# Silu of queries, keys and values as one ScalarE function into SBUF, with two gate results issued earlier

## The reference

```python
qkv = jax.nn.silu(hidden_states @ qkv_w.T)        # silu(a) = a * sigmoid(a); then q, k, v of each head
# per head: scores = (q k^T) * decay, causal; attended = scores v
normed = norm_w * attended * rsqrt(mean(attended ** 2) + eps)
gate = jax.nn.sigmoid(hidden_states @ gate_w.T)
out = gate * normed @ out_w.T
```

## Time and profile before

| | |
|---|---|
| time, median of 3 runs (range) | 1873.34 us (1871.03 to 1873.51) |
| span of the profiled execution, first to last instruction | 1870.5 us |
| own time of the profiled execution | not recorded apart; its span is 2.84 us under the median |
| TensorE busy | 1807.6 us (97%) |
| VectorE busy | 1443.7 us (77%) |
| ScalarE busy | 940.1 us (50%) |
| GpSimd busy | 627.6 us (34%) |
| chain that ended last: TensorE, VectorE, ScalarE | 77%, 13%, 4% |
| TensorE's granted clock, mean | 0.992 |

### The profile page before, as it was taken

The page is one execution under the profiler, slowest core; times in us unless marked ns, Lnnn a source line. Parts: engine busy times, 40 slices in busy tenths (PEclk is TensorE's granted clock), DMA queues, the critical chain, the costliest instruction groups (busy, mean ns, idle before and its releaser), DMA issues.

```text
span 1870.5 us, 26340 instructions
## 1 busy us (share of the span) xinstructions
PE 1807.6 (97%) x9325; PEld 872.7 (47%) x9325; DVE 1443.7 (77%) x2029; ACT 940.1 (50%) x1402; POOL 627.6 (34%) x506
## 2 busy tenths in 40 slices
PE   6999999999999999999999999999999999998887
PEld 4444544444444544444444544444444544564433
DVE  7777777778777777778777777778777777669877
ACT  5554544545454545545454545445354544434664
POOL 2352334324342334324342334324342332301423
PEclk9999999999999999999999999999999999999998
DMA  4112223131322223221321213121221213133332
GB/s 174 65 68 91 69 90 90 69 90 46 119 63 90 69 89 91 76 83 46 119 62 57 70 56 90 57 68 46 85 63 57 71 54 91 58 103 122 113 91 90
DMA packets 117792, 149.64 MB, mean 80 GB/s; under 512 B 67232, under 2 KB 83744, under 8 KB 117280
## 3 DMA queue, kind: packets, MB, share of 16 engines
q1 hardware_dynamic: 106208, 135.29, 22.9%
q0 software_dynamic: 2560, 8.39, 1.4%
q10 hardware_dynamic: 8896, 4.28, 0.8%
HBM read 119.63 MB, written 12.58 MB: 71 GB/s over the span
## 4 chain that ended last, share of the span: by engine, by line
PE 77%; DVE 13%; ACT 4%; issue 4%; DMA 1%; POOL 0%; ACTq 0%; DVEq 0%; SPq 0%; POOLq 0%
PE bank L1296 18%; PE bank L1298 17%; PE bank L1297 17%; PE bank L1269 6%; PE bank L1361 4%; PE bank L1363 3%; PE bank L1362 3%; DVE gated_split L1616 3%; PE bank L1338 2%; PE bank L1340 2%; PE bank L1339 2%; DVE acc L1758 2%; PE bank L1425 1%; PE bank L1436 1%; DVE bank L1676 1%
## 5 line engine op out<-in xcount | busy, mean ns | idle before, releaser
L1296 PE MATMUL bank<-x_blocks,w_pair 128*128 128x512 f16 (+1 forms) x1820 | 678.5, 373 | 12.7 <-DVE bank L1664 7.3
L1298 PE MATMUL bank<-x_blocks,w_pair 128*128 128x512 f16 (+1 forms) x1820 | 678.3, 373 | 0.0
L1297 PE MATMUL bank<-x_blocks,w_pair 128*128 128x512 f16 (+1 forms) x1820 | 678.2, 373 | 0.0
L1876 POOL TENSOR_TENSOR sums_pair<-raw_pair 128x512 f32<-128x512 f32 x63 | 87.0, 1380 | 576.5 <-DVE w_pair L1616 414.6
L1296 PEld LDWEIGHTS bank<-x_blocks,w_pair 128*128 128x128 f16 x1820 | 177.9, 98 | 218.2 <-DVE bank L1664 15.0
L1298 PEld LDWEIGHTS bank<-x_blocks,w_pair 128*128 128x128 f16 x1820 | 178.0, 98 | 202.8
L1297 PEld LDWEIGHTS bank<-x_blocks,w_pair 128*128 128x128 f16 x1820 | 178.1, 98 | 191.0
L1758 DVE TENSOR_TENSOR acc<-acc,bank 128x512 f32<-128x512 f32 x320 | 207.8, 680 | 17.5 <-PE bank L1363 17.5
L1537 ACT ACTIVATE scores_split<-bank 128x512 f16<-128x512 f32 (+1 forms) x192 | 100.6, 526 | 180.9 <-DVE bank L1721 160.7
L1616 DVE SCALAR_TENSOR_TENSOR w_pair<-raw_pair,w_pair 128x1024 f16<-128x1024 f32 x126 | 158.0, 1273 | 34.3 <-ACT w_pair L1489 34.1
L1902 POOL TENSOR_TENSOR ssq<-ssq,sig 128x512 f32<-128x512 f32 x64 | 83.4, 1303 | 282.4 <-ACT sig L1543 281.9
(11 more groups left out here) (212 smaller groups left out, 2637.4 us busy)
## 6 DMA issues: line engine op xcount, KB each, us to landing
raw_pair<-w_qk SPq DMA_DIRECT2D x32, 1024.0 KB, 5.0
raw_pair<-w_gate SPq DMA_DIRECT2D x16, 1024.0 KB, 4.9
raw_pair<-w_out SPq DMA_DIRECT2D x16, 1024.0 KB, 4.9
raw_pair<-w_vt SPq DMA_DIRECT2D x15, 1024.0 KB, 4.9
decay_sb<-decay SPq DMA_DIRECT2D x32, 256.0 KB, 5.3
raw_pair<-ctx_in SPq DMA_DIRECT2D x8, 1024.0 KB, 4.8
acc<-x_t SPq DMA_DIRECT2D x4, 1024.0 KB, 11.5
ctx<-raw_pair SPq DMA_DIRECT2D x8, 512.0 KB, 3.4
```

The source lines that it names most:

```text
L1296: pe.matmul(out, w_hi, x_hi, start=unmet and k == 0, stop=False, skip_group_check=halves or not fresh)
L1297: pe.matmul(out, w_hi, x_lo, start=False, stop=False, skip_group_check=halves or not fresh)
L1298: mm = pe.matmul(out, w_lo, x_hi, start=False, stop=k == QT - 1, skip_group_check=halves or not fresh)
```

## The change

The Silu of a q, k or v quarter becomes one ScalarE instruction, the function Silu, from bank or `p_copy` into the fp32 SBUF tile `sig`. The multiplication on VectorE is gone. High and low half are made from `sig` instead of from the bank. The bank is released once Silu has read it; the `sig` tile is held until the low half is made. Besides, the last two gate results of a pair (`gate_rest`: gate(3), gate(2)) move from after product 6 of the query stage to after product 1, ahead of unit 3's split and of the first query result. The pair n = 15 had them there before. `kv_out`, `v_out` and `end_v` change as `qk_out` does below.

```diff
@@ def silu(self, done, place, sign, dst, dst_free):
-        st = self.add("silu", done=done, place=place, sign=sign, gi=gi, sig_free=self.sig_free[gi], sig=self.tick("sig"),
-                      silu=self.tick("silu"), dst=dst, free=dst_free if isinstance(dst_free, list) else [dst_free],
+        st = self.add("silu", done=done, place=place, sign=sign, gi=gi, sig_free=self.sig_free[gi], silu=self.tick("silu"),
+                      dst=dst, free=dst_free if isinstance(dst_free, list) else [dst_free],
                       slot=self.late_slot, hi=self.tick("qkv_hi"))
-        self.sig_free[gi] = st["silu"]
-        return self.tick("qkv_lo")
+        lo = self.sig_free[gi] = self.tick("qkv_lo")
+        return st["silu"], lo
@@ def qk_out(self, which, r):
-        lo = self.silu(done, place, sign, (which, r), [self.qk_free, self.g_split] if which == "k" else self.qk_free)
-        self.release(place, lo)
+        silu, lo = self.silu(done, place, sign, (which, r), [self.qk_free, self.g_split] if which == "k" else self.qk_free)
+        self.release(place, silu)
@@ main_part, query stage of pairs 1 to 14
-            "p1": [attend(3), gated(3)] + units(3),
+            "p1": [attend(3), gated(3)] + gate_rest + units(3),
             "p2": sums(S2) + split_sum(S2) + stages(0) + sums(S1),
-            "p6": stages(1) + split_sum(S1) + sums(S4) + gate_rest + split_sum(S4),
+            "p6": stages(1) + split_sum(S1) + sums(S4) + split_sum(S4),
@@ scalar_program
         elif kind == "silu":
-            src = c.placed(st["place"])
             act.wait_ge(sem[st["done"][0]], st["done"][1])
             until(act, sem, st["sig_free"])
-            act.activation(c.sig32[st["gi"]][:, :], src, ACT.Sigmoid, scale=st["sign"] / W_SCALE).then_inc(sem["sig"])
+            act.activation(c.sig32[st["gi"]][:, :], c.placed(st["place"]), ACT.Silu,
+                           scale=st["sign"] / W_SCALE).then_inc(sem["silu"])
+            src = c.sig32[st["gi"]][:, :]
             act.wait_ge(sem["silu"], st["silu"][1])
@@ vector_program
         elif kind == "silu":
-            src = c.placed(st["place"])
-            dve.wait_ge(sem["sig"], st["sig"][1])
-            dve.scalar_tensor_tensor(out=src, in0=src, scalar=st["sign"] / W_SCALE, in1=c.sig32[st["gi"]][:, :],
-                                     op0=ALU.mult, op1=ALU.mult).then_inc(sem["silu"])
+            src = c.sig32[st["gi"]][:, :]
             dve.wait_ge(sem["qkv_hi"], st["hi"][1])
```

More of the change, by code:

```diff
@@ L63 @@
 SEMAPHORES = (
-    ["const_in", "ones_set", "constants", "quant_set", "x_hi", "x_lo", "w_hi", "w_lo", "sig", "silu", "qkv_hi", "qkv_lo",
+    ["const_in", "ones_set", "constants", "quant_set", "x_hi", "x_lo", "w_hi", "w_lo", "silu", "qkv_hi", "qkv_lo",
      "gate_sig", "score_mm", "decayed", "s_hi", "s_lo", "attend_mm", "sq", "gated", "g_sum", "g_hi", "g_lo", "ssq", "out_mm", "out_seeded",
@@ L340, in kv_out @@
         done, place, sign = self.result(r)
-        lo = self.silu(done, place, sign, ("kv", b, r), [self.qk_free, self.g_split, self.late_units_free])
-        self.release(place, lo)
+        silu, lo = self.silu(done, place, sign, ("kv", b, r), [self.qk_free, self.g_split, self.late_units_free])
+        self.release(place, silu)
         self.qk_done[("k", r // 2, b)] = lo
@@ L351, in v_out @@
         done, place, sign = self.result(r)
-        lo = self.silu(done, place, sign, ("v_unit", r), self.s_free if r == 0 else self.vo_free)
-        self.release(place, lo)
+        silu, lo = self.silu(done, place, sign, ("v_unit", r), self.s_free if r == 0 else self.vo_free)
+        self.release(place, silu)
         self.add("v_turn", r=r, ready=lo, free=max(self.v_hl_free))
@@ L386, in end_v @@
         bank = v["banks"][half]
-        done = self.silu(v["mm"][half], bank, 1.0, ("v", v["b"], half), self.v_hl_free[v["b"]])
+        silu, done = self.silu(v["mm"][half], bank, 1.0, ("v", v["b"], half), self.v_hl_free[v["b"]])
         self.v_done[v["b"]] = [[done]] * GH
-        self.main_ring.give(bank, done)
+        self.main_ring.give(bank, silu)
     def values(self, b):
```

## The result

The changed kernel takes 1891.59 us (median of 4 runs, 1890.04 to 1892.46) against 1872.31 for the kernel before on the same chip: ratio 1.0102, 95% interval 1.0088 to 1.0116. The forecast was 1895, 1.2% slower, with a range of 1870 to 1905. VectorE lost 87.6 us of busy time and TensorE did the same work; the kernel became 19 us slower. The 192 multiplications alone were 133 us, so the VectorE instructions that stay took some 45 us longer. TensorE's granted clock is no part of the 19 us: it is 0.992 on average in both, and ahead of the last 20 us it stood at its lower level, 1.2 GHz, for 13.7 us in all in each of the two profiled executions.

The account below looks back on a forecast made before the run. TensorE, busy 97% of the span, was taken as the bound, its waits set by VectorE's order of work. (2.1 - 0.43) x 14 = +23.4, less 1.3, gives +22; 1870.5 + 22 + 2.84 = 1895 us, range 1870 to 1905.

Parts of the forecast that it names:

- Table loads: ScalarE, before gate 0, q0 and gates 2 to 15: 30 more loads, 39 us of ScalarE; gate loads hidden.
- Rival (a): Silu shares Sigmoid's table set, no added loads, GpSimd turns stay: +0.4 to +0.9 us a pair, 1877 to 1885; chance 0.15.
- rival (d): A change of table costs twice its row, draining included: 1.28 x 14 us more, 1913; chance 0.05.
- Turns with GpSimd: Query stage: VectorE splits with both inputs in SBUF alternate with GpSimd's instructions; product 5 starts 2.1 us later per pair.
- The sign named for it: TensorE's wait for u3 grows from 0.45 to over 2 us a pair, some at the out product behind S2's split.
- Key stage and last pair: Key stage: wait for line 1758 goes, -0.43 x 14 = -6.0 us; last pair's seed wait: -1.3 us.
- The sum: (2.1 - 0.43) x 14 = +23.4, less 1.3: +22 us on the span of 1870.5.
- The last stretch: Last pair: a seed costs TensorE 2.14 us, its high half waited 1.42 for the multiplication; gain -1.3 us.
- Rival (b): Loads added, but low halves keep 0.69 us: (0.34 - 0.43) x 14 - 1.3 = -2.6, 1871; chance 0.13.
- Rival (c): Neither loads nor GpSimd turns: product 5 0.28 us sooner, key stage's 0.43 gone, -11 us, 1862; chance 0.10.
- The move: Query stage: two gate results wait for unit 3's gating; alone expected at +0.5 to +1.3 us a pair, 1879 to 1891.

Follow-up runs that it names:

- in-place kernel: The changed kernel with Silu written back into the PSUM bank (or copy of product 7) it reads, both halves made from there: 1864.09 us, ratio 0.9956.
- the kernel with both: The changed kernel with the activation written back where it reads, and Sigmoid where Silu stands (multiplication by the argument left out): 1861.61 us, ratio 0.9946.
- the kernel with only q0 in place: The changed kernel with only the first query quarter of pairs 1 to 15 written back into its bank and split there: 1868.87 us, ratio 0.9979.

## Why the prediction was right, point by point

- **Table loads: right.** 30 more, at the places named (Silu's line is 1524 in the changed kernel, not 1525), 1.283 us each, the next activation 0.01 to 0.02 us behind. Rival (a)'s set and rival (d)'s doubling are out. No draining of 1.38 us, as the Trainium skill has it (ScalarE: Activation LUTs, "What ACT_TABLE_LOAD costs"), is to be seen: the load's whole effect on the chain was 6.95 - 5.54 = 1.41 us, the load and the 0.1 us by which neighbouring activations otherwise overlap. The load before the gate results was hidden, as said: the Square after it had no idle time before it any more, but started in time.
- **Turns with GpSimd: right in kind.** q0's low half took 1.21 us, S2's split 1.75, and with the bank as source 0.69 and 0.68. With the order of the prediction, product 5 was to start 2.1 us later; it was 13.97 - 12.06 = 1.91. The steps on the way fit: in the clock of before, S2's split ended at 1083.65 (forecast 1083.6), the three additions at 1085.45 (1085.4), u3 at 1088.96 (1089.2). The sign named for it, a wait for u3 of over 2 us with some of it at S2, came with other shares: 0.30 at the seed, 1.15 at S2, 0.57 at u3, 2.0 in all.
- **Key stage and last pair: right.** The wait for line 1758 is gone (-0.43 us a pair), the last seed wait fell from 2.14 to 0.67 us, -1.5 for -1.3.
- **The sum:** (1.91 - 0.43) x 14 = +20.7, for +23.4 predicted. One term was missing and one sized too small:
- **Before pair 1, not in the sum.** The changed kernel is 1.9 us late: TensorE waits there 2.42 us for c22 at 56.61, after ScalarE waited 3.35 for GpSimd's first weight sums. It was 1.44 us in the in-place kernel. The rows of VectorE and GpSimd show turns again, of another split: without the multiplications VectorE reaches two splits of weights, both inputs in SBUF, 2.5 us sooner (47.04, before 49.57), beside GpSimd's sums. They take 4.48 us for 2.83 before (3.51 in place), GpSimd's last two sums 2.13 each for 1.27. No run moves these splits alone.
- **The last stretch, sized too small.** From pair 15 on it gave back 4.9 us by difference (17.4 = 1.9 + 20.4 - 4.9), of which the seed is 1.5. Of the other 3.4, some 2.6 stand at line 1269, where TensorE waited 3.5 us behind VectorE before and 0.9 now; multiplications left VectorE there too. The rest are small waits in both directions.
- **How near 1895 came.** In spans the forecast was +22.1 and the result +17.4: the pairs cost 3.0 less and the last stretch gave back 3.6 more than forecast, against the 1.9 before pair 1. That 1895 came as near as 3.4 us is in part luck: these errors cancel in part, and the new median lies 3.7 us above its profiled span where I added 2.84.
- **Rival (a), priced wrong.** I gave no loads with turns 1877 to 1885; measured 1868.08. S2's split was right (1082.4 against 1075.05 + 7.18 = 1082.23), the step behind it was not. The prediction doesn't write it out; for product 5 at 1087.9 or later, S1's and S4's splits had to meet one GpSimd sum more than before; it started at 1075.05 + 12.43 = 1087.48, as the two splits took 2.86 us for 2.87. What remained, +0.37 - 0.43, is nothing, and the end gave the rest.
- **Rival (b), right in kind.** Loads with low halves of 0.69 us: +0.34 - 0.43 a pair predicted, +0.18 - 0.43 measured; 1871 for 1864.09, the difference mostly in the same last stretch.
- **Rival (c): the number met, by another way.** Neither load nor turns is the kernel with both: 1861.61 for 1862. But product 5 started only 0.04 us sooner, not 0.28, as S4's split still stood ahead of u3; a pair won 0.50 us, not 0.71, and the last stretch gave the rest. With S4's split behind u3 product 5 did start 0.24 sooner (11.82 after the Square).
- **The move: overpriced** where I took it by itself (1879 or more, 1874.74 measured), since the split that it delays drops out of GpSimd's way. The forecast's own working had this 0.69, and was right.

## What to carry to other kernels

Price a delay against the moment at which its result is wanted, and all delays on one chain together: here each of two fitted into 1.4 us of slack and cost some 2 and 6.5 us in all, the pair of them 29, and both fitted again once the moved gate results went back. An instruction saved on a busy engine is worth what the bound engine waited for it, while the instructions that stay may get slower by their new operands: where a low half moves from PSUM to SBUF, look at what GpSimd does at that moment. If functions of two table sets must alternate, put the change where ScalarE idles anyway, even at the price of one old-style operation; here the number of loads (1, 31 or 59) didn't set the time, their places did.

## What the runs showed of the hardware that I had not expected

A table load doesn't wait for the data of the activation it stands before: it ran 3.46 us ahead of it (978.47 and 981.93 above). And the values' first quarter, its low half now with both inputs in SBUF, took 1.70 us in each of the 14 pairs, where GpSimd's sums ran beside it. It cost nothing: the kernel with only q0 in place keeps it, and its pairs are as long as with all in place (instructions on tile sig, changed kernel: count, shortest/median/longest ns):

```profile
L1617 DVE SCALAR_TENSOR_TENSOR scores_split<-sig,scores_split x14: 1695/1699/1704, 192.2 to 1578.2; 128x512 f16<-128x512 f32 x14
L1617 DVE SCALAR_TENSOR_TENSOR w_vo<-sig,w_vo x42: 691/692/693, 201.7 to 1592.1; 128x512 f16<-128x512 f32 x42
```

The 42 others of the value stage, with GpSimd idle, stayed at 0.69. That fits the Trainium skill's rule of ports held for a whole instruction (SBUF — State Buffer, "two separate sides").
